# Reordering the start of a selective-scan pass and its handover to an attention pass

## The chip, the cores and the metric

The kernel runs on one core of one Trainium2 chip. A core has five instruction queues: TensorE (PE in the profile), VectorE (DVE), ScalarE (ACT), GpSimd (POOL) and SyncE (SP), which here issues all DMAs. The engines work side by side and wait for each other by semaphores. The metric is the device time of one execution, in microseconds (us).

## The reference

One decoder layer on x of 8 sequences of 512 tokens with 256 features, in float32:

```python
x = x + mamba_block(layernorm(x))                    # L0_attn
x = x + cross_attention(layernorm(x), ctx_1024, ...) # 16 heads of 16
x = x + spiking_ffn(layernorm(x))

def mamba_block(x):
    x_norm = layernorm(x)
    y = (mamba(x_norm, "f") + flip(mamba(flip(x_norm), "b"))) / 2
    x = x + y
    return x + w2 @ gelu(w1 @ layernorm(x) + b1) + b2

def mamba(x):                                        # inner width 512, 16 states
    xi, z = split(x @ in_w.T)
    u = silu(causal_conv4(xi) + conv_b)
    dt, B, C = split(u @ xp_w.T)
    delta = softplus(dt @ dt_w.T + dt_b)
    h[t] = exp(delta[t] * A) * h[t-1] + delta[t] * u[t] * B[t]
    y[t] = sum_n h[t, n] * C[t, n] + u[t] * D
    return (y * silu(z)) @ out_w.T
```

## The kernel before

There are two passes. The first, `mamba_pass`, does the two scans of each sequence. The second, `attention_pass`, does the block's feed-forward part, the cross attention and the spiking part. The first writes its result to DRAM (`mid`), the second loads it.

**Scan pass.** A unit is one sequence in one direction, 16 in all; a loop body holds two units. A unit is 4 blocks (`k`) of 128 channels by 8 pairs of states, 32 steps `p`. A step is:

- `decay` on ScalarE: two exponentials dA of 128x511, from delta.
- `spread_du` on TensorE: the products delta·u·B into a PSUM `pair` bank. 16 small matmuls take `duT` (the transposed product delta·u) and `diagB[:, j]`, diagonals that hold B of the pair j.
- `scan` on VectorE: two scans of 128x512, from dA and the pair bank into h.
- `weigh` on GpSimd: h times the broadcast C (`C_rep`) into hC; `sum_states` on TensorE sums hC into `y_bank`.

The next unit's projections stand between the steps, at places given by small tables (`XI_AT`, `Z_AT` and so on). Three PSUM banks (`general`) are handed out in turn by a `Ring`, along a list of keys (`mamba_keys`, `attention_keys`): a key's first matmul waits until the key before it in that bank has been read.

**Ahead of the loop** stands the first unit's preparation, written out in order on every engine: load x, normalise it twice (VectorE has the statistics, GpSimd the root, ScalarE the scaling), transpose, project xi (keys `xi`, 0 to 3) and gate's z (`z`, 0 to 3), convolve (`start_conv` on ScalarE, three `tap`s on VectorE), silu of all of u and all of z (`silu`), `x_proj`, copy xd (`take_xd`), B (`take_bt`), delta (`soft`, `make_delta`), the product du (`make_du`) and its transposes (`du_rows`, `take_du`). Eight diagonals are made, four on ScalarE (32 small activations) and four on GpSimd. The next unit's first blocks are projected too: z 0 to 2 and xi 0 (keys `("z", 4)` to `("z", 6)` and `("xi", 4)`). At last comes the first spread. Before its loop TensorE waits until the last three keys of the list are read.

**Handover.** At the end of the scan pass TensorE works ahead on the first sequence's feed-forward part (`first_up`, with `first_gelu` on ScalarE), projects the last output (`out_proj`), VectorE adds it to `res` (`add_out`) into `x_out`, and SP stores it as the last slot of `mid`. Each of the five engines then adds one to `handover`, and each waits for all five before it starts on the attention pass. There VectorE first sets constants (`ones_bf`, three rows of `k_st`, `v_sb`), adds the feed-forward result (`add_down`), normalises (`xn_q`), and prepares q, k and v and the masks. SP writes q and k, each cut into three bf16 parts (`cut_lo`, `cut_last`), to DRAM in six DMAs and reads them back in stacked form (`stacks`). After that TensorE starts the loop: `prescore` is a head's four score tiles, of which VectorE takes the maxima with `mask_bias`. `x0` (also `x_mid`) and `xn` belong to the next sequence's feed-forward part, normalised by `first_norm(1)`. `start_x1n` and `take_x1` are sums of 128x1024 on GpSimd.

## Time and profile before

| | |
|---|---|
| median of 3 runs | 2777.25 us (2776.8 to 2777.51) |
| the profiled execution | 2776.59 us, span 2774.8 us |
| TensorE busy | 2633.1 us, 95% |
| VectorE busy | 2203.8 us, 79% |
| ScalarE busy | 1743.1 us, 63% |
| GpSimd busy | 1715.4 us, 62% |
| granted TensorE clock, mean | 0.98 of full |

The span runs from the first instruction to the last. Busy shares are averages over stages with different limits. A line of the timeline is a start, a length, the engine and line of the code, what is written from what, how often, and in brackets the idle time ahead of it with what ended it. A matmul of float32 data shows as two instructions. All instructions made by a helper carry the helper's line: L467 and L471 are the scan pass's matmuls and transposes, L698 its activations, L1325 and L1333 the attention pass's matmuls and transposes, L1236 its DMA issues.

### The profile page before, as it was taken

The numbers are of one execution on the slowest core, as the hardware profiler recorded it, in microseconds if no ns is written. First come the engines' busy times: TensorE is split into PE (matmuls) and PEld (weight loads), VectorE is DVE, ScalarE is ACT, GpSimd is POOL, SyncE is SP. The second block draws the span as 40 slices with busy tenths as digits, with TensorE's granted clock in tenths as the row PEclk, the third lists the DMA queues.
The fourth block names the chain that finished last, engine by engine and source line by source line (L and its number), as shares of the span: only waits on it lengthen the run. The fifth ranks groups of instructions, "written<-read, shape, count | busy, mean of one in ns | idle before, by whom it ended". The sixth has DMA issues, their size and how long they took to land. (4 is left out here: it accounts for less than half of the span.)

```text
span 2774.8 us, 55530 instructions
## 1 busy us (share of the span) xinstructions
PE 2633.1 (95%) x19210; PEld 1798.9 (65%) x19210; DVE 2203.8 (79%) x3271; ACT 1743.1 (63%) x2899; POOL 1715.4 (62%) x962
## 2 busy tenths in 40 slices
PE   5999999999999999999999878999999999999996
PEld 2787787787787778877887744455554545454523
DVE  3999999999999899999999959584848484858573
ACT  4778878877877888788778423535354544444342
POOL 1898989988988998899899812323233232323130
PEclk9999999999999999999999989999999999999978
DMA  3122121302221221222122052304040404040300
GB/s 122 33 80 81 63 65 65 103 28 78 88 67 54 79 81 48 79 66 95 36 77 101 9 158 78 99 25 116 8 121 2 121 2 121 2 121 2 106 2 15
DMA packets 102089, 187.07 MB, mean 67 GB/s; under 512 B 14720, under 2 KB 75264, under 8 KB 100256
## 3 DMA queue, kind: packets, MB, share of 16 engines
q1 hardware_dynamic: 101840, 183.92, 21.3%
q8 instruction: 135, 2.21, 0.3%
q14 instruction: 114, 0.93, 0.1%
HBM read 148.38 MB, written 35.52 MB: 66 GB/s over the span
## 5 line engine op out<-in xcount | busy, mean ns | idle before, releaser
L1087 POOL TENSOR_TENSOR hC<-h,C_rep 128x1024 f32<-128x1024 f32 x512 | 1201.3, 2367 | 100.6 <-DVE h L945 94.1
L945 DVE TENSOR_TENSOR_SCAN h<-dA,pair 128x512 f32<-128x512 f32 x1024 | 1171.3, 1201 | 107.8 <-PE pair L467 96.5
L698 ACT ACTIVATE dA<-delta,cols 128x511 f32<-128x511 f32 x1024 | 664.1, 711 | 41.7 <-DVE h L945 28.3
L467 PE MATMUL pair<-diagB,duT 64*128 64x128 f32 x8192 | 549.0, 281 | 23.4 <-DVE h L945 15.2
L467 PEld LDWEIGHTS pair<-diagB,duT 64*128 64x128 f32 x8192 | 486.2, 188 | 124.5 <-issue 92.7
L558 PE MATMUL y_bank<-ident,hC 128*128 128x128 f32 x4112 | 537.3, 277 | 5.5 <-POOL hC L1087 4.5
L558 PEld LDWEIGHTS y_bank<-ident,hC 128*128 128x128 f32 x4112 | 456.3, 141 | 97.7 <-issue 55.7
L1820 DVE CUSTOM_DVE_ANT_0 masked<-pair,mask_bias 128x512 f32<-128x512 f32 x512 | 322.2, 686 | 19.1 <-PE pair L1325 13.5
L1563 ACT ACTIVATE pr<-pair 128x1024 f32<-128x1024 f32 x256 | 248.3, 1021 | 74.3 <-PE pair L1325 74.3
L1922 POOL CAST m_part<-m_rest 8x512 bf16<-8x512 f32 x16 | 9.6, 602 | 429.1 <-ACT m_rest L1563 429.1
L467 PE MATMUL general<-xnT,w_in 128*128 128x512 f32 x512 | 250.5, 605 | 10.9 <-ACT zs L698 5.1
L1944 POOL TENSOR_TENSOR pr<-pr,keep_word 128x512 int32<-128x512 int32 x112 | 163.9, 1466 | 116.5 <-ACT pr L1563 114.2
L1325 PE MATMUL general<-w_down,g 128*128 128x256 f32 x1024 | 232.5, 380 | 2.8 <-DVEq L1655 2.8
L1325 PEld LDWEIGHTS general<-w_down,g 128*128 128x128 f32 x1024 | 193.7, 190 | 34.8 <-issue 3.8
L1325 PE MATMUL pair<-q_st,k_st 99*128 99x512 bf16 x512 | 196.2, 383 | 3.5 <-ACT pr L1563 3.5
L1325 PE MATMUL general<-xT,w_up 128*128 128x512 f32 x360 | 168.3, 605 | 1.2 <-ACT xT L1563 0.7
L1325 PE MATMUL pair<-k_st,q_st 96*128 96x512 bf16 x512 | 151.5, 404 | 9.1 <-DMA q_st<-qk_parts 6.2
L955 DVE SCALAR_TENSOR_TENSOR u<-general,cols,u 128x511 f32<-128x511 f32 (+2 forms) x192 | 141.9, 739 | 22.8 <-ACT u L698 18.8
L1325 PE MATMUL pair<-mask_biasT,ident_bf 128*128 128x512 bf16 x400 | 152.6, 382 | 0.0
L1893 POOL TENSOR_SCALAR rstd<-mv 128x4 f32<-128x4 f32 x24 | 15.6, 650 | 199.0 <-DVE mv L1670 196.4
L1325 PEld LDWEIGHTS pair<-q_st,k_st 99*128 99x128 bf16 x512 | 50.1, 98 | 135.9 <-ACT pr L1563 91.0
L1078 POOL TENSOR_TENSOR ab<-delta,u 128x512 f32<-128x512 f32 x64 | 82.0, 1281 | 81.6 <-DVE delta L936 81.6
(177 smaller groups left out, 3166.8 us busy)
## 6 DMA issues: line engine op xcount, KB each, us to landing
C_rep<-c_rows SPq DMA_DIRECT2D x128, 512.0 KB, 4.3
qk_parts<-qk_part SPq DMA_DIRECT2D x96, 256.0 KB, 3.9
w_in<-w_in SPq DMA_DIRECT2D x16, 1024.0 KB, 4.9
k_st<-qk_parts SPq DMA_DIRECT2D x8, 1536.0 KB, 9.1
q_st<-qk_parts SPq DMA_DIRECT2D x8, 1536.0 KB, 9.2
x_in<-x SPq DMA_DIRECT2D x18, 512.0 KB, 5.3
w_out<-w_out SPq DMA_DIRECT2D x17, 512.0 KB, 4.2
mid<-x_out SPq DMA_DIRECT2D x9, 512.0 KB, 4.7
```

Of the source, the lines that this page charges most:

```text
L467: return pe.matmul(o, lhsT, rhs, start=start, stop=stop)
L558: last = pe.matmul(y_bank[:, c * P:(c + 1) * P], hC[:, g % RING, i, c * P:(c + 1) * P], ident[:, :], start=j == 0 and i == 0 and c == 0, s ...
L698: return act.activation(o, i, fn, **kw)
L945: last = dve.tensor_tensor_scan(h[:, g % 4, i, :], dA[:, g % 4, i, :], dBu[:, i, :], 0.0, ALU.mult, ALU.add)
L955: dve.scalar_tensor_tensor(u[n][:, k, lag:T], raw[:, 0:T - lag], col("fb"[n] + "conv_w", CW * k + CW - 1 - lag), u[n][:, k, lag:T], ALU.mu ...
L1078: pool.tensor_tensor(ab[:, :], delta[:, k % 2, :], u[par][:, k, :], ALU.mult).then_inc(s_du.sem, 1)
L1087: pool.tensor_tensor(hC[:, g % RING], h[:, g % 4], C_rep[:, 2 * j:2 * j + 2, :], ALU.mult).then_inc(s_hC.sem, 1)
L1325: return pe.matmul(o, lhsT, rhs, start=start, stop=stop)
L1563: return act.activation(o, i, fn, **kw)
L1820: dve.tensor_tensor_reduce(masked[:, j % 2, :], bank[j], mask_bias[:, j, :], 1.0, FLOOR, ALU.add, ALU.max, m_col[:, j, hd:hd + 1]).then_in ...
L1893: pool.tensor_scalar(rstd[:, :], mv[:, :, 1], EPS, None, ALU.add)
L1944: pool.tensor_tensor(words, words, keep_word[:, unit % 2, :].unsqueeze(1).broadcast_to((P, len(heads), T)), ALU.mult).then_inc(s_kept.sem, 1)
```

## The change

No loop body is changed in what it computes or in its order; one wait is added in VectorE's attention code for the first sequence. Parts of the start of the scan pass and of the handover stand in another order or on another engine.

- Start: VectorE negates A_log behind the first statistics. Gate's four blocks of the first unit go to the four `pair` banks, off the ring. ScalarE applies silu to u block by block, and `x_proj` waits for each block (`first_silu`). All eight diagonals are made by GpSimd, two of them ahead of du. The second unit's first blocks `("xi", 4)` and `("z", 4)` are projected ahead of du's transposes, `("z", 5)` and `("z", 6)` behind the first spread, and ScalarE copies those two between its first decays.
- Handover: the last output projection and its two adds move into the attention pass (`last_out` on TensorE, `add_last` on VectorE, keys `lo`), the store behind the stacks of q and k. The ones in `k_st` are written by ScalarE. In `attention_keys` v's projection comes last, behind q's. VectorE's preparation stands in another order. `take_x1(0)` waits until `mask_bias` is set. `yT`, `w_out` and `res` outlive the first pass, so some tiles of the second lie at other addresses; `mask_i` now lies on `x1` and `x_res`.

TensorE from the first projections to the first spread, before and then after. The names: `general` and `pair` are PSUM banks; `xnT` is the normed input, `xd_sb` the result of x_proj, `ab` du, `hC` the states' sums (zero here).

```order
L467 MATMUL general<-xnT,w_in 128x512 x16
L467 MATMUL general<-u_64,w_xp 64x256 x8
L471 MATMUL general<-ident,xd_sb 128x128 x4
L467 MATMUL general<-xd_sb,w_dt 128x512
L467 MATMUL general<-xnT,w_in 128x512 x8
L467 MATMUL y_bank<-hC,ident 128x512
L471 MATMUL general<-ident,ab 128x128 x4
L467 MATMUL pair<-diagB,duT 128x64x2 x8
```

```order
L475 MATMUL general<-xnT,w_in 128x512 x6
L475 MATMUL pair<-xnT,w_in 128x512 x4
L475 MATMUL general<-xnT,w_in 128x512 x2
L475 MATMUL pair<-xnT,w_in 128x512 x4
L475 MATMUL y_bank<-hC,ident 128x512
L475 MATMUL general<-u_64,w_xp 64x256 x8
L479 MATMUL general<-ident,xd_sb 128x128 x4
L475 MATMUL general<-xd_sb,w_dt 128x512
L475 MATMUL general<-xnT,w_in 128x512 x4
L479 MATMUL general<-ident,ab 128x128 x4
L475 MATMUL pair<-diagB,duT 128x64x2 x8
L475 MATMUL general<-xnT,w_in 128x512 x4
```

The z blocks stand in pair banks between the xi blocks, the matmul on `y_bank` has moved ahead of x_proj, and two of the next unit's four blocks (of two matmuls each) have moved behind the spread.

ScalarE in the same stretch, before and then after. `u_64` and `zs_63` are u and z of the forward direction, `zs_65` z of the backward one.

```order
L698 ACTIVATE u_64<-general,cols 128x512 x4
L698 ACTIVATE zs_63<-general 128x512 x4
L698 ACT_TABLE_LOAD
L698 ACTIVATE u_64<-u_64 128x2048
L698 ACTIVATE zs_63<-zs_63 128x2048
L732 ACT_TABLE_LOAD
L698 ACTIVATE xd_sb<-general,cols 64x256 x2
L698 ACTIVATE BT<-general 64x4x16 x2
L698 ACTIVATE ab<-general 128x512
L698 ACTIVATE ab<-ab 128x512 x2
L698 ACTIVATE diagB<-eye,BT 128x64 x32
L698 ACTIVATE zs_65<-general 128x512 x3
```

```order
L718 ACTIVATE u_64<-general,cols 128x512 x3
L718 ACTIVATE zs_63<-pair 128x512 x2
L718 ACT_TABLE_LOAD
L718 ACTIVATE u_64<-u_64 128x512
L718 ACTIVATE u_64<-general,cols 128x512
L718 ACTIVATE zs_63<-pair 128x512
L718 ACTIVATE u_64<-u_64 128x512
L718 ACTIVATE zs_63<-pair 128x512
L718 ACTIVATE u_64<-u_64 128x512 x2
L718 ACTIVATE zs_63<-zs_63 128x2048
L862 ACT_TABLE_LOAD
L718 ACTIVATE xd_sb<-general,cols 64x256 x2
```

The one silu of 128x2048 on u became four of 128x512, which stand between the copies; the 32 activations on `diagB` are gone.

TensorE over the handover, before and then after; the unconditional branches are the boundary of the two passes.

```order
L467 MATMUL pair<-xT_57,w_up_54 128x512 x10
L467 MATMUL general<-w_out,yT 128x256 x16
L330 UNCONDITIONAL_BRANCH
L1320 UNCONDITIONAL_BRANCH
L1325 MATMUL general<-w_down_53,g_58 128x256 x32
L1325 MATMUL general<-ctxT,w_att 128x512 x2
L1325 MATMUL y_bank<-ctxT,w_att 128x512 x2
L1325 MATMUL general<-w_att,ctxT 128x256 x8
L1325 MATMUL pair<-keep_bf,ones_bf 128x512 x4
L1333 MATMUL general<-ident,xn_q 128x128 x4
L1333 MATMUL y_bank<-ident,xn_q 128x128 x4
L1325 MATMUL general<-xT_57,w_att 128x512 x4
```

```order
L1364 UNCONDITIONAL_BRANCH
L1369 MATMUL general<-w_down_53,g_58 128x256 x32
L1369 MATMUL general<-ctxT,w_att 128x512 x2
L1369 MATMUL y_bank<-ctxT,w_att 128x512 x2
L1369 MATMUL general<-w_out,yT 128x256 x8
L1377 MATMUL general<-ident,xn_q 128x128 x8
L1369 MATMUL pair<-keep_bf,ones_bf 128x512 x4
L1369 MATMUL y_bank<-xT_57,w_att 128x512 x2
L1369 MATMUL general<-xT_57,w_att 128x512 x2
L1369 MATMUL general<-w_out,yT 128x256 x8
L1369 MATMUL general<-w_att,ctxT 128x256 x4
L1369 MATMUL y_bank<-w_att,ctxT 128x256 x4
```

The 16 matmuls on `w_out` stood ahead of the boundary and stand in two groups of 8 behind it; those of v (`w_att,ctxT` 128x256) moved to the end.

The diff, cut to its core:

```diff
-    before = many("w2", 2) + many("k", KD) + many("v", 2) + many("qn", KD) + many("q", KD)
+    before = many("w2", 2) + many("k", KD) + [("lo", 0)] + many("qn", KD) + many("q", KD) + [("lo", 1)] + many("v", 2)
...
-    before = [("nf", k) for k in range(KD)] + [("xi", k) for k in range(KI)] + [("z", k) for k in range(KI)]
+    before = [("nf", k) for k in range(KD)] + [("xi", k) for k in range(KI)]
     before += [("xd", 0), ("bt", 0), ("dt", 0)]
-    before += [("z", KI + k) for k in range(KI - 1)] + [("xi", KI), ("tr", 0)]
+    before += [("xi", KI), ("z", KI), ("tr", 0)] + [("z", KI + k) for k in range(1, KI - 1)]
...
+            def first_z(k):
+                for kk in range(KD):
+                    last = mm(bank[k][:, :], w_in[:, kk, DI + k * P:DI + (k + 1) * P], xnT[:, kk, :], kk == 0, kk == KD - 1)
+                last.then_inc(G.full_sem(("z", k)), 1)
...
+                if isinstance(b, str) and b == BEFORE:
+                    pe.wait_ge(first_silu.sem, first_silu.count(kk))
+                elif kk == 0:
                     pe.wait_ge(u_silu.sem, u_silu.count(X))
...
+            du_rows(0, 0, 0, BEFORE)
+            pe.wait_ge(kinds["z"][1].sem, kinds["z"][1].count(KI - 1))
+            spread_du(0, 0)
+            for k in range(1, KI - 1):
                 for kk in range(KD):
                     in_proj(("z", KI + k), 1, 0, k, kk, BEFORE)
...
-            for jj in range(TT // 2):
-                for half in range(2):
-                    out_proj(jj, half, TT + jj, 2 * B - 1, AFTER)
             settle(pe)
             pe.sem_inc(handover.sem, 1)
...
+            for k in range(2):
+                first_z(k)
+            first_u(0)
+            start_conv(KI - 1, 0, 0, KI - 1, BEFORE)
+            first_z(2)
+            first_u(1)
+            first_z(3)
+            for k in range(2, KI):
+                first_u(k)
+            act.wait_ge(kinds["z"][1].sem, kinds["z"][1].count(KI - 1))
+            f(zs[0][:, :, :], zs[0][:, :, :], ACT.Silu).then_inc(z_silu.sem, 1)
+            act.preload_act_table_set("natural_log_exp_and_others")
...
-            for j in DIAG_ACT:
-                diagonals(0, j)
-            for k in range(KI - 1):
-                take_z(KI + k, 1, 1, k, BEFORE)
             start_conv(KI, 1, 1, 0, BEFORE)
+            take_z(KI, 1, 1, 0, BEFORE)
             take_du(0, 0, 0, BEFORE)
+            act.wait_ge(setup.sem, setup.count(0))
+            decay(0, 0, 0)
+            take_z(KI + 1, 1, 1, 1, BEFORE)
+            decay(0, 0, 1)
+            take_z(KI + 2, 1, 1, 2, BEFORE)
+            decay(0, 0, 2)
...
-            for jj in range(TT // 2):
-                dve.wait_ge(s_mid.sem, s_mid.count(B - 1))
-                add_out(jj, TT + jj, x_out, AFTER)
...
+            def first_diagonals(js):
+                for j in js:
+                    made = diag_pool if j in DIAG_POOL else diag_act
+                    pool.wait_ge(kinds["bt"][1].sem, kinds["bt"][1].count(0))
+                    pool.tensor_tensor(diagB[:, j], eye_all(), b_all(j), ALU.mult).then_inc(made.sem, 1)
+            first_diagonals((0, 1))
             make_du(0, 0, 0)
-            for j in DIAG_POOL:
-                diagonals(0, j)
+            first_diagonals(range(2, NP))
...
-            sp.wait_ge(early.mid.sem, early.mid.count(B))
             x_used(0)
             load_x(1)
             dma(s_mask, mask_i[:, :, :], a["mask"].rearrange("(j p) t -> p j t", p=P))
             stacks(0, 0)
             stacks(1, 0)
+            sp.wait_ge(kinds["lo"][1].sem, kinds["lo"][1].count(1))
+            dma(early.mid, mid[B * TT:(B + 1) * TT].rearrange("j p f -> p j f"), early.tiles[0][:, :, :])
...
+            act.wait_ge(s_ones.sem, s_ones.count(0))
+            f(k_st[6 * DH:QR, :, :].rearrange("p h (c e) -> p (h c) e", e=P),
+              ones_bf[6 * DH:QR, :].unsqueeze(1).broadcast_to((3, H * TT, P))).then_inc(k_ones.sem, 1)
...
-            dve.memset(k_st[6 * DH:QR, :, :], 1.0)
...
+            dve.drain()
+            take_q(BEFORE)
+            cut_lo(0, 1)
+            dve.tensor_scalar(keep[:, :, :], maskT_i[:, :, :], 0.0, MASKED, ALU.is_equal, ALU.mult)
+            cut_last(0, 1)
+            add_last(1)
+            first_norm(1)
+            dve.drain()
+            dve.tensor_tensor(mask_biasT[:, :, :], keep[:, :, :],
+                              not_full[:, :].unsqueeze(1).broadcast_to((P, TT, T)), ALU.mult)
             for jj in range(TT // 2):
                 take_v(jj, BEFORE)
...
+            pool.wait_ge(setup_dve.sem, setup_dve.count(1))
             take_x1(0)
```

## Rows read from the trace of the kernel before

**Rows 1.** Scan-loop stretches (width; PE, PEld, DVE, ACT, POOL busy; clock; DMA; GB/s).
```profile
69.30:165.00 95.70, 92.61 (x889) 75.56 (x890) 89.21 (x103) 78.64 (x142) 82.50 (x45) 1.00 0.20 64
...
261.00:357.00 96.00, 93.61 (x895) 75.97 (x894) 89.51 (x102) 78.40 (x142) 86.22 (x48) 1.00 0.23 74
```

**Rows 2.** Issues of the first microsecond (size, us to landing); VectorE's timeline (start, us).
```profile
x_in<-x SPq DMA_DIRECT2D x1, 512.0 KB, 4.0
...
6.45 1.40 DVE L912 BATCH_NORM_STATS2 stats<-x_in 128x6 f32<-128x256 f32 x4
```

**Rows 3.** Timeline of ScalarE and TensorE, gate's projections to xd.
```profile
30.64 0.78 ACT L698 ACTIVATE u<-general,cols 128x512 f32<-128x512 f32 x1 [0.94 <-PE general L467]
...
32.35 0.78 ACT L698 ACTIVATE u<-general,cols 128x512 f32<-128x512 f32 x1 [0.94 <-PE general L467]
...
41.89 1.28 ACT L698 ACT_TABLE_LOAD   x1
43.18 1.91 ACT L698 ACTIVATE u<-u 128x2048 f32<-128x2048 f32 x1
...
45.19 3.62 PE L467 MATMUL general<-u,w_xp 128*64 128x256 f32 x16 [4.07 <-issue]
...
48.91 0.95 ACT L698 ACTIVATE xd_sb<-general,cols 64x256 f32<-64x256 f32 x2 [0.71 <-PE general L467]
```

**Rows 4.** Timeline of the diagonals, and the stretch of the blocks behind them.
```profile
53.50 7.73 ACT L698 ACTIVATE diagB<-eye,BT 128x64 f32<-128x64 f32 x32
...
55.64 4.72 POOL L1093 TENSOR_TENSOR diagB<-eye,BT 128x512 f32<-128x512 f32 x4
...
62.00:66.00 4.00, 4.00 (x6) 1.68 (x7) 0.00 (x0) 0.97 (x3) 0.00 (x0) 0.54 0.55 224
```

**Rows 5.** Timeline of TensorE and VectorE, first pairs of the loop.
```profile
71.75 1.16 PE L467 MATMUL pair<-diagB,duT 64*128 64x128 f32 x16 [0.79 <-DVE h L945]
...
76.45 1.16 PE L467 MATMUL pair<-diagB,duT 64*128 64x128 f32 x16
...
78.45 4.54 DVE L945 TENSOR_TENSOR_SCAN h<-dA,pair 128x512 f32<-128x512 f32 x4
```

**Rows 6.** Timelines at the handover: last gelu on ScalarE, first attention matmul on TensorE.
```profile
1610.15 0.69 ACT L698 ACTIVATE g<-pair,cols 128x512 f32<-128x512 f32 x1 [1.03 <-PE pair L467]
...
1619.81 14.05 PE L1325 MATMUL general<-w_down,g 128*128 128x256 f32 x64 [2.79 <-DVEq L1655]
```

**Rows 7.** Timelines of TensorE and of SP's queue; last row an issue's landing.
```profile
1645.08 5.37 PE L1325 MATMUL general<-xT,w_att 128*128 128x512 f32 x8 [2.59 <-DVE v_sb L1713]
...
1644.36 3.47 SPq L1236 DMA_DIRECT2D qk_parts<-qk_part  x6
1650.75 0.33 SPq L1236 DMA_DIRECT2D k_st<-qk_parts  x1
1655.96 3.46 SPq L1236 DMA_DIRECT2D qk_parts<-qk_part  x6
1663.93 0.33 SPq L1236 DMA_DIRECT2D q_st<-qk_parts  x1
...
q_st<-qk_parts SPq DMA_DIRECT2D x1, 1536.0 KB, 9.3
```

**Rows 8.** Timeline of VectorE, between handover and prescores.
```profile
1638.95 1.38 DVE L1677 TENSOR_SCALAR xn_q<-x1n,mv,rstd 128x256 f32<-128x256 f32 x4 [1.30 <-POOL rstd L1895]
...
1659.52 5.51 DVE L1677 TENSOR_SCALAR xn<-x_mid,mv,rstd 128x256 f32<-128x256 f32 x4 [1.64 <-POOL rstd L1895]
1665.13 3.33 DVE L1801 TENSOR_SCALAR keep<-mask_i 128x2048 f32<-128x2048 int32 x1
```

**Rows 9.** Timelines of TensorE and VectorE, first head of the prescores.
```profile
1673.33 1.89 PE L1325 MATMUL pair<-k_st,q_st 96*128 96x512 bf16 x4 [6.20 <-DMA q_st<-qk_parts]
...
1679.21 1.88 PE L1325 MATMUL y_bank<-xT,w_up 128*128 128x512 f32 x4
...
1676.46 0.63 DVE L1820 CUSTOM_DVE_ANT_0 masked<-pair,mask_bias 128x512 f32<-128x512 f32 x1
```

More of the change, by code:

```diff
@@ L169, in batch @@
         return keys
-    return before, apart(batch(4)), apart(batch(2) + [("yb", 2 * KI)] + [("op", TT + jj) for jj in range(TT // 2)])
+    return before, apart(batch(4)), apart(batch(2) + [("yb", 2 * KI)])
 BEFORE, AFTER = "before", "after"
@@ L988, in add_out @@
                                   ALU.add).then_inc(G.done_sem(("op", i)), 1)
+            first, second = norm_steps(0)
+            for fn in first:
+                fn()
             dve.wait_ge(a_log.sem, a_log.count(0))
@@ L994, in _ @@
             last.then_inc(setup.sem, 1)
-            first, second = norm_steps(0)
-            for fn in first:
-                fn()
             dve.memset(hC[:, :, :, :], 0.0)
@@ L1122, in _, with attention_pass @@
             pool.sem_inc(handover.sem, 1)
-def attention_pass(nc, ctx, a, mid, out, sb, where, stage, psum, consts, handover, early):
+    return Late(yT, w_out, res)
+def attention_pass(nc, ctx, a, mid, out, sb, where, stage, psum, consts, handover, early, late):
     f32, bf16, i32 = mybir.dt.float32, mybir.dt.bfloat16, mybir.dt.int32
@@ L1478, in spike_input, with last_out @@
                 last.then_inc(G.full_sem(key), 1)
+            def last_out(jj):
+                key = ("lo", jj)
+                pe.wait_ge(*G.free(key, BEFORE))
+                bk = G.bank(key, BEFORE)
+                for half_ in range(2):
+                    j = 2 * jj + half_
+                    for k in range(KI):
+                        last = mm(bk[:, half_ * D:(half_ + 1) * D], late.yT[:, k, j * P:(j + 1) * P], late.w_out[:, k, :],
+                                  k == 0, k == KI - 1)
+                last.then_inc(G.full_sem(key), 1)
             pe.wait_ge(early.down.sem, early.down.count(0))
```

99 lines of the change are left out of this document (55 added, 44 removed).

## The prediction

> **What bounds the kernel now.** Read first the page's busy shares: TensorE is busy 95% of the span, the others 62 to 79%. Then stretches of the scan loop: 96 us from the first scan on and 96 us two units later look alike, TensorE busy 92.6 and 93.6 us, at the full granted clock [rows 1]. So the loop runs at its own pace from its first pair on. The change touches no loop body of either pass; what it saves ahead of a loop moves the whole loop, and is kept to the end if the loop starts in the same pattern. Only two serial stretches matter, then: the start (0 to 78 us) and the handover from scan to attention (1610 to 1679 us). There I read the timelines engine by engine, and at each start what released it.
>
> **The start, step by step.**
> - The first statistics. x_in is the first load (issued at 0.8) and lands 4.0 later, at 4.8; VectorE begins at 6.45, behind the negation of A_log [rows 2]. The negation moves behind the statistics: up to 1.6 earlier. The memset of hC then ends about when ScalarE's first normed tile is ready, so I take 1.5, for all as far as the third xi block (its copy moves from 30.64 to 29.1).
> - Projections. Blocks leave TensorE 1.71 apart (30.64 and 32.35) [rows 3]. In the pair banks gate's blocks wait for no general bank: z0 is ready at 30.9, z1 32.6, xi3 34.3, z2 36.0, z3 37.7. ScalarE copies z1 until 33.2, loads its table (1.28) until 34.5, then alternates silu of one block (0.65 each, a third of the 1.91 for four since part of that is fixed) with conv3 (0.78) and two copies (0.6): silu u0 ends 35.1, u1 37.2, u2 38.9, u3 39.6. Gate's silu (1.9) and the second table load end at 42.8. TensorE's x_proj (3.62) runs beside, 38.4 to 42.0. So xd is copied from 42.8 instead of 48.91: 6.1 gained. ScalarE is last here, by 0.8.
> - Diagonals and du. ScalarE worked 7.73 on its four diagonals, three copies of z came after, TensorE stood waiting for these and did the next blocks at a granted clock of 0.54, the 1.2 GHz level [rows 4]. Now ScalarE makes none. GpSimd makes eight at 1.18 (4.72 for four): two from 45.3, du from 48.3 to 49.6 (6.8 behind xd's copy, as before), six until 56.7. Each is ready ahead of its spread; the last one only holds GpSimd's first weighing, at 56.7 instead of 71.7. du's transposes end at 50.3, its copy at 51.0, and the first scan starts at about 52.4 instead of 69.3.
> - What is given back. z5 and z6 are now projected behind the first spread and copied between decays: z5's copy starts at 54.1, decay 1 ends 56.0, z6's copy 56.6. TensorE waits for that copy ahead of its loop, and behind this wait every spread of the loop is queued. With 0.8 for entering the loop (an estimate from the 0.8 of issue that stood ahead of spread 1 before) spread 1 starts at 57.4, spread 2 at 58.5 against 71.75, spread 3 4.70 later, as before: 63.2 against 76.45 [rows 5]. Its scan starts at 64.5 instead of 78.45, 14.0 earlier. TensorE's own chain is 13.3 earlier at spread 3 and 13.6 at spread 4, which no longer waits. I take 13.7. Had all followed the first scan it would be 16.9; were each silu and copy 0.15 dearer and the loop entered 0.5 later, about 12. Bounds 12 to 16.
>
> **The handover.**
> - The last gelu ends at 1610.84, attention's first matmul starts at 1619.81 [rows 6]: out_proj, its two adds and the store of x_out stand between. They go behind the handover, and TensorE's down projection starts 8.4 earlier, at 1611.4. The loads issued at the handover move with it. Setting three rows of k_st to one moves from VectorE to ScalarE: four times the 2048-column pass is 7.6 us, and ScalarE has nothing to do until k is projected, behind the down projection's 14 us: nothing.
> - k. Its parts are cut 8.3 earlier (1636.1), the read of k_st is issued at 1642.4 instead of 1650.75 [rows 7].
> - q. Its projection started at 1645.08 after waiting 2.59 for VectorE's copy of v, and took 5.37 with one more wait. Now it takes banks that are free earlier, and v comes last: it starts when the normed query is copied, 1635.2, and ends 3.4 later, 1638.6. last_out(0), 3.5 us, lies in the time in which TensorE waited for the normed query; last_out(1) behind q. Cutting q followed 5.5 behind the projection's end, so it ends at 1644.2 instead of 1655.96: 11.7.
> - The queue. q's six writes ended at 1663.93, 4 us behind the end of k_st's read (1650.75 plus 9.2, the like read of q_st taking 9.3). Two loads issued right behind q_st's read didn't lengthen it [rows 7]. Both look like one queue served in order. So now k_st lands at 1651.7, q's writes end at 1655.7, q_st lands 9.3 later at 1665.0, against 1673.3: only 8.3; 3.4 of q's gain is lost in the queue.
> - VectorE. Beside GpSimd's sums the four rows of xn took 5.51 and keep 3.33, alone the four of xn_q 1.38, and the other keep of this size takes 1.2 [rows 8]. take_x1 now waits behind mask_bias, so GpSimd is quiet: 6.2 less. From q's cut to the first maximum it was 20.5; less 6.2, and 5.0 more for last_out's add, mask_biasT, v and keep_word, 19.3: ready at 1663.5 instead of 1676.46. The transfer is last now, no longer VectorE.
> - Into the loop. TensorE began the prescores at 1673.33, VectorE joined at 1676.46 [rows 9], and TensorE waited for it in the second head. Now VectorE is there first and TensorE sets the pace (from the lower clock again after some 9 idle us). The second head's prescores are done at 1670.2 instead of 1679.21: **9.0**. Without the last 0.7 it is 8.3; were VectorE last still, 1676.46 to 1663.9 would be 12.6. Bounds 8 to 12.6.
>
> One rule bears on the moved take_x1. The Trainium skill, "SBUF — State Buffer", on who interferes with whom, says that VectorE and GpSimd share a port pair as an exclusive lock, the loser blocked for the whole instruction. The trace agrees (5.51 for four rows beside GpSimd, 1.38 alone). [...]
>
> The sum: 2776.6 (the profiled execution; its span is 2774.8) - 13.7 - 9.0 = 2753.9. The median of the runs is 0.66 above that execution, so the time is 2754.5. At the bounds: 2777.25 - 28.6 = 2748.7 and 2777.25 - 20 = 2757.3.
>
> **Rivals.**
> 1. The queue isn't in order: q's writes share the engines with k_st's read and end 6.4 behind their start, as k's did (1644.36 to 1650.75 [rows 7]). q_st lands at 1660 and VectorE is last: 12.6 instead of 9.0, 2751.0. Against it: the reading of the queue above. Chance 0.15. The Trainium skill, "DMA: Bandwidth & Descriptors", on HWDGE ordering, says that each DMA engine consumes descriptors in ring order but that completion is not first-in first-out; the trace goes with the first half.
> 2. TensorE falls to the lower level in the start. Before, 4.07 idle us ahead of x_proj left it fast [rows 3], some 5 ahead of the later blocks did not (0.54 [rows 4]). The gaps forecast are 2 us or less, but more of them. At the lower level x_proj costs 3.6 more, the two blocks ahead of du hold it up by 2.5, and z5 with z6 cost 2 to 3: the start gives 5 instead of 13.7, time 2763. A part of it gives 2757 to 2760. Chance 0.13 for both.
> 3. Slower. The first pairs enter the loop with another distance (12.1 us from scan 0 to scan 3, where it was 9.15), and the loop keeps a worse pattern, TensorE and VectorE waiting for each other at each pair. It decides from 22.7 us over 512 pairs, 44 ns a pair; at 100 ns it costs 51 and the time is 2806. Against it: the two stretches of [rows 1] are alike although one comes from the start and the other from a loop's end. Chance 0.04.
> 4. The change doesn't do what it says: a load that doesn't move (C_rep, weights) absorbs it, 2772 to 2782. Against it: C_rep is issued 6 us earlier, at 45.8, and first used at 56.7. Chance 0.04.
>
> The forecast has 0.64. Range 2748.5 to 2761: the forecast, rival 1 and the mild half of rival 2. About 0.2% (5.5 us) is what a measurement of this kernel tells from no change: faster 0.93 (forecast, rivals 1 and 2, part of 4), same 0.03, slower 0.04.
>
> **What would show it.** In the profile after: xd copied at 42.8 with two table loads ahead of it, not more; scan 0 near 52.4 and spread 3 near 63; 53.6 us (before 53.5) between attention's first matmul and its first prescore, which q_st's read releases; q's writes 11.4 us long, not 8; xn at 0.35 a row. I am wrong in the start if scan 0 comes early and spread 3 doesn't, in the handover if VectorE or k_st's constants are last, and altogether if a unit of the loop isn't 95.8 us.

## The result and the profile after

The kernel after takes 2754.98 us (median of 6 runs, 2752.52 to 2756.8), the kernel before beside it 2777.2: a ratio of 0.992, 95% interval 0.9908 to 0.9932. In a later set of runs (run 12 below) it was 2754.68 (5 runs) against 2777.3, ratio 0.9918 (0.9904 to 0.9931). 2754.5 was forecast.

| profiled execution | before | after |
|---|---|---|
| time, span | 2776.59, 2774.8 | 2753.38, 2751.6 |
| xd copied from | 48.91 | 41.28 |
| scan 0, scan 3 | 69.30, 78.45 | 52.98, 64.83 |
| spread 3 | 76.45 | 63.55 |
| last gelu's start | 1610.15 | 1597.75 |
| attention's first matmul | 1619.81 | 1599.01 |
| first prescore | 1673.33 | 1651.71 |
| second head's up projection | 1679.21 | 1657.31 |

**The start.** ScalarE's timeline (start, length) beside [rows 3]: the first table load, silu of the first block of u, the second table load, the copy of xd.

```profile
32.01 1.28 ACT L718 ACT_TABLE_LOAD   x1
...
33.30 0.63 ACT L718 ACTIVATE u<-u 128x512 f32<-128x512 f32 x1
...
39.99 1.28 ACT L862 ACT_TABLE_LOAD   x1
41.28 0.95 ACT L718 ACTIVATE xd_sb<-general,cols 64x256 f32<-64x256 f32 x2
```

Two table loads as before, but the first comes 9.9 earlier and silu starts on one block. Then TensorE, from x_proj to spread 3, in the places of [rows 3, 4, 5] (after x_proj: xd's transposes, dt, the two blocks, the first spread, spreads 1 and 2, spread 3):

```profile
37.29 1.95 PE L475 MATMUL general<-u,w_xp 128*64 128x256 f32 x16
...
42.38 1.10 PE L479 MATMUL general<-ident,xd_sb 128*128 128x128 f32 x4 [3.14 <-ACT xd_sb L718]
43.27 1.92 PE L475 MATMUL general<-xd_sb,w_dt 81*128 81x512 f32 x2
44.98 5.30 PE L475 MATMUL general<-xnT,w_in 128*128 128x512 f32 x8
...
51.71 1.16 PE L475 MATMUL pair<-diagB,duT 64*128 64x128 f32 x16 [0.96 <-ACT duT L718]
...
57.95 2.06 PE L475 MATMUL pair<-diagB,duT 64*128 64x128 f32 x32 [1.45 <-ACT zs L718]
...
63.55 2.06 PE L475 MATMUL pair<-diagB,duT 64*128 64x128 f32 x32
```

and the granted clock of that stretch (the number behind the busy times of PE, PEld, DVE, ACT and POOL):

```profile
41.00:46.00 5.00, 3.62 (x8) 2.10 (x9) 0.00 (x0) 2.45 (x7) 1.84 (x2) 0.56 0.57 170
46.00:51.00 5.00, 4.75 (x12) 2.06 (x10) 1.71 (x3) 2.57 (x5) 3.54 (x4) 0.76 1.01 329
```

TensorE stood idle for 3.14 us ahead of the transposes and came back at the 1.2 GHz level: dt took 1.92, the two blocks 5.30. x_proj took 1.95, where it took 3.62 before [rows 3]. Both are 16 instructions of one form, and in the loop it takes 1.95 as well. The granted clock under the 3.62 of before:

```profile
45.20:48.80 3.60, 3.60 (x16) 1.87 (x16) 0.00 (x0) 2.97 (x2) 0.00 (x0) 0.53 0.49 175
```

So before the change x_proj ran at the lower level, behind 4.07 idle us. VectorE's scans:

```profile
52.98 2.33 DVE L981 TENSOR_TENSOR_SCAN h<-dA,pair 128x512 f32<-128x512 f32 x2 [0.65 <-PE pair L475]
...
64.83 4.55 DVE L981 TENSOR_TENSOR_SCAN h<-dA,pair 128x512 f32<-128x512 f32 x4 [0.39 <-PE pair L475]
```

Scan 0 is 16.3 earlier, scan 3 13.6, spread 3 12.9.

**The loop.** In the stretches of [rows 1] TensorE is now busy 94.3 and 94.6 us (92.6 and 93.6), the clock at 1.00. The higher number comes from where the window falls: in the 95.7 us from the first scan on, as in the first of [rows 1], it is 92.8. Its pace is best read from the loads of w_in, one for each unit; the first and last start of these on SyncE, before and then after:

```profile
L337 SPq DMA_DIRECT2D w_in<-w_in x16: 373/383/434, 2.8 to 1365.1; - x16
```

```profile
L346 SPq DMA_DIRECT2D w_in<-w_in x16: 373/384/434, 2.8 to 1352.6; - x16
```

Of the sixteen, fourteen are issued in the loop, from 119.64 before and from 106.03 after. That is 95.81 us a unit before and 95.89 after. So the 13.6 us by which the first of these loads is earlier are 12.46 at the last, and the last gelu is 12.4 earlier. The missing 1.2 is taken up again below.

**The handover.** Last gelu, then TensorE at the down projection, the q projection (its first row), the first prescore and the second head's up projection, beside [rows 6, 7, 9]:

```profile
1597.75 0.69 ACT L718 ACTIVATE g<-pair,cols 128x512 f32<-128x512 f32 x1 [1.03 <-PE pair L475]
```

```profile
1599.01 14.05 PE L1369 MATMUL general<-w_down,g 128*128 128x256 f32 x64 [1.29 <-DVEq L1717]
...
1622.77 1.98 PE L1369 MATMUL y_bank<-xT,w_att 128*128 128x512 f32 x4 [1.09 <-ACT xT L1622]
...
1651.71 1.88 PE L1369 MATMUL pair<-k_st,q_st 96*128 96x512 bf16 x4 [7.95 <-DMA q_st<-qk_parts]
...
1657.31 1.88 PE L1369 MATMUL y_bank<-xT,w_up 128*128 128x512 f32 x4
```

SyncE's issues, beside those of [rows 7], and VectorE's xn, keep and first maximum, beside [rows 8, 9]:

```profile
1623.57 3.48 SPq L1279 DMA_DIRECT2D qk_parts<-qk_part  x6
1629.55 0.33 SPq L1279 DMA_DIRECT2D k_st<-qk_parts  x1
1631.99 3.19 SPq L1279 DMA_DIRECT2D qk_parts<-qk_part  x6
1642.63 0.33 SPq L1279 DMA_DIRECT2D q_st<-qk_parts  x1
```

```profile
1636.16 1.38 DVE L1739 TENSOR_SCALAR xn<-x_mid,mv,rstd 128x256 f32<-128x256 f32 x4 [1.64 <-POOL rstd L1967]
...
1642.00 1.23 DVE L1871 TENSOR_SCALAR keep<-mask_i 128x2048 f32<-128x2048 int32 x1
...
1652.50 0.69 DVE L1890 CUSTOM_DVE_ANT_0 masked<-pair,mask_bias 128x512 f32<-128x512 f32 x1 [1.53 <-issue]
```

The down projection starts 20.8 earlier, which is the 12.4 of the last gelu and 8.4. q is projected 22.3 earlier (1622.77 against 1645.08), but q's writes need 10.6 from issue to end, and q_st's read, the last thing that TensorE waits for (7.95 idle), lets it go only 21.6 earlier. VectorE's four rows of xn took 1.38 (before 5.51), keep 1.23 (3.33).

**The end.** The store of the last but one sequence's output is issued at 2683.43 (before 2705.07), 21.6 earlier; from there to the end it is 68.2, before 69.7.

### The profile page after: what moved, and what is told of

The parts are those of the page before. It is cut to its first block and busy times, and to the rows that moved or that the text cites. A ratio compares the mean times of both kernels' runs of the same rounds, so it can differ in the third digit from the quotient of the medians.

```text
span 2751.6 us, 55456 instructions
## 1 busy us (share of the span) xinstructions
PE 2626.7 (95%) x19177; PEld 1797.4 (65%) x19210; DVE 2191.5 (80%) x3270; ACT 1743.0 (63%) x2871; POOL 1720.0 (63%) x966
## 5 line engine op out<-in xcount | busy, mean ns | idle before, releaser
L475 PE MATMUL pair<-diagB,duT 64*128 64x128 f32 x8192 | 549.7, 281 | 23.3 <-DVE h L981 13.7
L475 PE MATMUL general<-xnT,w_in 128*128 128x512 f32 x496 | 242.0, 603 | 4.5 <-ACT xnT L718 3.6
L1369 PE MATMUL pair<-mask_biasT,ident_bf 128*128 128x512 bf16 x368 | 140.6, 382 | 0.0
L1369 PEld LDWEIGHTS pair<-k_st,q_st 96*128 96x128 bf16 x512 | 50.2, 98 | 116.4 <-DVE m_col L1890 82.1
```

The costliest lines, as they stand in the source:

```text
L475: return pe.matmul(o, lhsT, rhs, start=start, stop=stop)
L1369: return pe.matmul(o, lhsT, rhs, start=start, stop=stop)
```

## The experiments

Runs of one chip are compared with each other: before took 2778.0 beside the first four kernels, 2776.63 beside the next four, 2777.3 beside the last. The kernel after alone spread over 4.3 us in its six runs, so where a kernel has a single run (3, 4, 6, 7, 8) its time says little, and the argument rests on its profile. A profile is one execution: kernels with the same code up to there copied xd at 40.81 (run 4) to 42.38 (run 8).

**1. The start alone.** The handover stands as before.

```
- attention_keys, last_out, add_last, take_x1's wait   (as in the kernel before)
+ first_silu, first_z, first_diagonals, z5/z6 behind the first spread   (as in the kernel after)
```

> The start's changes alone; the handover as before. If the gain is the sum of two independent stretches, spread 3 stands at 63.5 as in the changed kernel (76.45 before), the time is 2777.2 less 12.4 to 13.6: 2763.6 to 2764.8, and the stretch from last gelu to the second head's products is as before (68.4 us from 1610.84 to 1679.21). Rival, one part needs the other: then it is more than 1.5 us outside this. A second question: w_in's issues in the scan loop were 13.6 earlier in unit 0 and 12.5 earlier in the last one. If the start's pattern costs this, it is here too; if it belongs to single executions, it may be absent.

Measured: 2766.79 (5 runs, 2766.15 to 2767.28), ratio 0.996 (0.9946 to 0.9974): 11.2 less than before, where 12.4 to 13.6 were expected. Spread 3 stands at 63.50, as in the kernel after, and from the last gelu's end to the second head's up projection it is 68.5 us (before 68.4). The difference went later: the last w_in is issued at 1353.47, only 11.6 earlier than before (95.96 us a unit), and the down projection follows it by 255.9, before by 254.7.

**2. The handover alone.** The start stands as before.

```
+ attention_keys, last_out, add_last, take_x1's wait   (as in the kernel after)
- first_silu, first_z, first_diagonals, z5/z6 behind the first spread   (as in the kernel before)
```

> The handover's changes alone; the start as before. Sum of two stretches: down projection 8.4 behind the last gelu less than before, prescores 9.2 earlier, second head's products 9.5 earlier, time 2767.7 (2767 to 2768.7). Rival, one part needs the other: over 1.5 us outside. The scan loop's w_in issues then stand where they stood before (119.6 and 1365.1); if they drift here by 1 us as well, the drift is not the start's.

Measured: 2768.4 (6 runs, 2767.63 to 2769.4), ratio 0.9965 (0.9953 to 0.9978): 9.6 less. The down projection follows the last w_in by 246.4 (before 254.7): the 8.3 to 8.4 again. Counted from there, the first prescore is 9.1 earlier, as expected, and the second head's up projection 8.4, not 9.5: its first up projection ran at the lower clock (3.62). The loop stands at 95.81 us a unit, so the 0.09 belongs to the start. The two parts give 20.8 when added, both together 22.2, a difference that the intervals don't resolve.

**3. Silu of u in one piece again.**

```
-            first_u(0)
             start_conv(KI - 1, 0, 0, KI - 1, BEFORE)
             first_z(2)
-            first_u(1)
             first_z(3)
-            for k in range(2, KI): first_u(k)
+            act.wait_ge(s_tap.sem, ...)
+            f(u[0][:, :, :], u[0][:, :, :], ACT.Silu).then_inc(first_silu.sem, KI)
```

> Silu on all of u in one activation again, and x_proj behind it, gate's blocks still in the pair banks. Theory (ScalarE is last here): the table load comes after z3's copy (37.1) unless the taps are later, u's silu 1.9 from 38.4 to 40.3, gate's 42.2, table 43.5; x_proj 40.3 to 42.3; so xd is copied at 43.5 instead of 41.28, 2.2 later, and the time is 2757. Rival, TensorE is last: x_proj ends before that and nothing beyond the two table loads matters, xd within 1 us of 41.28.

Measured: 2753.61 (one run), within the spread of the kernel after. ScalarE's copy of xd and TensorE's spread 3:

```profile
43.64 0.95 ACT L718 ACTIVATE xd_sb<-general,cols 64x256 f32<-64x256 f32 x2
```

```profile
64.93 2.06 PE L475 MATMUL pair<-diagB,duT 64*128 64x128 f32 x32
```

The step is right (xd 2.36 later, spread 3 1.38 later) and the time didn't follow. The last w_in comes at 1352.73, level with the kernel after's 1352.65: its loop took 95.79 us a unit, the other's 95.89, and 13 such units are the 1.3. So silu in blocks won nothing in the end.

**4. Four diagonals on ScalarE again.**

```
             soft(0, 0, 0, BEFORE)
+            for j in DIAG_ACT:
+                diagonals(0, j)
...
-            first_diagonals((0, 1))
             make_du(0, 0, 0)
-            first_diagonals(range(2, NP))
+            first_diagonals(DIAG_POOL)
```

> Four diagonals on ScalarE again (32 activations, 7.7 us), between delta's logarithm and the copy of xi 4; GpSimd makes four, behind du. Theory: copies of xi 4, z 4 and of du all wait for them: ScalarE is free at 47.2 + 7.7 = 54.9, du's copy ends about 57, scan 0 starts at 58 instead of 53.0, spread 3 about 5 later, time 2759.5 to 2760.5. Rival, the diagonals were hidden anyway behind du on GpSimd (done at 49.3): less than 2 us.

Measured: 2758.97 (one run), 4.0 more than the kernel after. TensorE ahead of its first spread:

```profile
55.05 2.08 PE L475 MATMUL pair<-diagB,duT 64*128 64x128 f32 x16 [6.67 <-ACT duT L718]
```

It waits 6.67 for ScalarE's copy of duT, which stands behind 7.76 us of diagonals. Scan 0 comes at 57.24 (4.3 later) and spread 3 at 69.48 (5.9 later). Of these 5.9 the faster loop returns 1.5 again (last w_in 4.4 later).

**5. The second table load behind the copies of xd.**

```
-            act.preload_act_table_set("natural_log_exp_and_others")
             act.wait_ge(s_zero.sem, s_zero.count(0))
             take_xd(0, BEFORE)
+            act.preload_act_table_set("natural_log_exp_and_others")
```

> The kernel after with one edit: ScalarE's second table load stands behind its copies of xd instead of ahead of them. Theory (after's trace: silu of z ends 39.97, the table load takes 1.28, xd is copied at 41.28, while x_proj ended at 39.2; TensorE then stood idle for 3.14 and did the next matmuls at the lower clock, dt's two in 1.92): the load is all that ScalarE holds up. xd is copied at 40.0, and TensorE idles 1.8 instead of 3.1. If the clock stays high with that, dt takes 1.0 and the two blocks 3.6, and scan 0 starts at about 50.8, time 2752.3. Rival: the clock falls as before; everything moves by 1.3 alone, scan 0 at 51.7, spread 3 at 62.3, time 2753.7. Second rival: GpSimd's diagonals hold spread 3 at 63 in any case, time as after (2755).

Measured: 2752.72 (4 runs, 2751.67 to 2755.05), ratio 0.9914 (0.9896 to 0.9932). The copy of xd, then TensorE's transposes and dt:

```profile
40.07 0.94 ACT L718 ACTIVATE xd_sb<-general,cols 64x256 f32<-64x256 f32 x2
```

```profile
41.15 0.72 PE L479 MATMUL general<-ident,xd_sb 128*128 128x128 f32 x4 [1.71 <-ACT xd_sb L718]
41.71 1.02 PE L475 MATMUL general<-xd_sb,w_dt 81*128 81x512 f32 x2
...
48.66 1.99 PE L475 MATMUL pair<-diagB,duT 64*128 64x128 f32 x16 [0.94 <-ACT duT L718]
50.58 4.49 PE L475 MATMUL general<-xnT,w_in 128*128 128x512 f32 x8
...
62.11 2.06 PE L475 MATMUL pair<-diagB,duT 64*128 64x128 f32 x32
```

The clock stays high after 1.71 idle us, dt takes 1.02 and scan 0 comes at 50.76, as expected for that case. But spread 3 gains 1.44 only. The lower level came later instead: the first spread took 1.99 (1.16 in the kernel after), and z5 with z6 4.49 (3.70), together 1.6 more. In run 11, with the same edit, these took 1.16 and 3.70, and spread 3 came at 59.74. Between the two runs the distance from xd's copy to spread 3 differs by the same 1.6. The time is 2.3 below the kernel after's 2754.98 of another set of runs, and the ranges of both overlap.

**6. Without z5 and z6.**

```
-            take_z(KI + 1, 1, 1, 1, BEFORE)
+            act.wait_ge(...); act.sem_inc(...)      # and on TensorE in_proj left out, the same for z6
             decay(0, 0, 1)
```

> Leaves out part of the computation: the second unit's gate blocks z5 and z6 are neither projected nor copied; their semaphores are stepped. It asks what gave back the difference between scan 0 (16.3 earlier than before) and spread 3 (12.9 earlier). Theory of the prediction: z5's and z6's projections (3.70) and copies do; without them spread 1 follows scan 0 at 53.7 instead of 57.95, and spread 3 would come up to 4.2 earlier, at 59.3. Rival, which I now hold likelier: behind spread 1 stand the sums of the first step, and GpSimd weighs that step only when its six diagonals are made (56.28, weighed at 58.64); so the sums start at 58.9 instead of 60.0, and spread 3 moves by 1.0 only, to 62.5, scan 3 to 63.8. Time 2754, or 2751 by the first theory.

Measured: 2748.78 (one run). TensorE's transposes, dt and spread 3:

```profile
41.91 0.72 PE L479 MATMUL general<-ident,xd_sb 128*128 128x128 f32 x4 [3.14 <-ACT xd_sb L718]
42.47 1.02 PE L475 MATMUL general<-xd_sb,w_dt 81*128 81x512 f32 x2
...
57.77 1.16 PE L475 MATMUL pair<-diagB,duT 64*128 64x128 f32 x16
```

Spread 3 is 5.8 earlier. 2.4 of that were there at scan 0 already (50.60): 0.5 at xd's copy (40.82), and 1.9 because dt and the blocks ran at the full clock although TensorE had been idle for the same 3.14. The other 3.4 are z5 and z6. The forecast's reason for what is given back between scan 0 and spread 3 stands, and the rival that I held likelier falls: the first sums came at 54.16, before GpSimd had weighed anything, so they don't wait for its diagonals. I had read the order of two rows as a dependence.

**7. q's writes ahead of both reads.**

```
+            for n in range(2): (three writes of part n)
+            sp.wait_ge(s_qkw.sem, s_qkw.count(1))
+            (read k_st; read q_st)
-            stacks(0, 0); stacks(1, 0)
```

> The kernel after with SyncE's order changed at the handover: k's three writes, q's three writes, then the two reads k_st and q_st behind each other (after: k writes, k_st read, q writes, q_st read; there q's writes took 10.6 from issue to end, the read before them 9, and q_st's read released TensorE at 1651.7). Theory, the queue is served in order: q's writes end about 6.3 behind their issue at 1632 (as k's do), so 1638.3 instead of 1642.6; both reads are then issued, k_st lands 9.0 later at 1647.3 and q_st 7.4 to 9.3 behind it, 1655 to 1656.6: TensorE's first prescore 3.3 to 5 later than 1651.7. Rival, reads share the sixteen engines: both land together at the end of the same time, which looks alike for the last one, but k_st lands late too, near 1655. A third, reads overlap: q_st lands 9.3 behind its issue, at 1647.6, 4.1 earlier than in after, and then VectorE (ready 1651.0) is last.

Measured: 2757.32 (one run), 2.3 more than after. SyncE's two reads, and TensorE's first prescore:

```profile
1638.26 0.33 SPq L1279 DMA_DIRECT2D k_st<-qk_parts  x1
1638.62 0.43 SPq L1279 DMA_DIRECT2D q_st<-qk_parts  x1
```

```profile
1654.98 1.88 PE L1374 MATMUL pair<-k_st,q_st 96*128 96x512 bf16 x4 [11.38 <-DMA q_st<-qk_parts]
```

q's writes, issued at 1631.9, have ended 6.4 later, not 10.6, when no read is ahead of them. By their landings k_st's read took 9.9 from its issue and q_st's 16.2, 6.7 behind it. That is one queue served in order: reads that share the engines would have landed together, overlapping reads at 1647.6.

**8. GpSimd's sums beside VectorE's preparation.**

```
-            pool.wait_ge(setup_dve.sem, setup_dve.count(1))
             take_x1(0)
+    ScalarE waits for mask_bias in their place; mask_i lies elsewhere, loaded behind w2
```

> The kernel after with GpSimd's sums of the next sequence (take_x1) not waiting for mask_bias: they stand beside VectorE's preparation again, as before the change (the int mask lies elsewhere and is loaded behind w2, and ScalarE's part of the loop waits for mask_bias in their place). Theory (before's trace: xn's four rows took 5.51 and keep 3.33 beside GpSimd; after's 1.38 and 1.23 without): VectorE is 6.2 later, ready at about 1657 instead of 1651.0, behind q_st's landing at 1651.7; the first maxima come at 1657.5 instead of 1652.5, and the second head about 5 later less what GpSimd's earlier end saves; time +3 to +5, 2758 to 2760. Rival: VectorE's slowness in before came from something else (its place in the order, the DMAs into the tiles); then xn takes 1.4 and the time stays at 2755.

Measured: 2758.67 (one run), 3.7 more. VectorE's rows of xn and the second keep:

```profile
1637.06 3.41 DVE L1741 TENSOR_SCALAR xn<-x_mid,mv,rstd 128x256 f32<-128x256 f32 x4 [1.64 <-POOL rstd L1969]
...
1648.60 3.33 DVE L1877 TENSOR_SCALAR keep<-mask_i 128x2048 f32<-128x2048 int32 x1
```

3.41 for 1.38 and 3.33 for 1.23, beside GpSimd's sums at 1637.3 and from 1645.2 to 1650.9. GpSimd, beside the first keep:

```profile
1645.18 3.19 POOL L1979 TENSOR_TENSOR x1n<-x_in,x_mid 128x1024 f32<-128x1024 f32 x1 [5.51 <-DVE keep_word L1869]
```

The first keep had started at 1644.93, ahead of this sum: it took its 1.23, and the sum 3.19 instead of 2.35. The second keep started behind a sum (1648.60 against 1648.51), and here VectorE paid. Whoever started second waited. VectorE's first maximum is 3.4 later (1655.92), 0.9 of it from ahead of the handover. The wait for mask_bias is worth this much, though in the kernel after VectorE isn't what TensorE waits for: without the wait it would be.

**9, 10. Reads cut by heads; then VectorE's closing memsets on GpSimd.**

```
-  read k_st; q's writes; read q_st
+  read k_st[heads 0:8]; q's writes; read q_st[heads 0:8]; read k_st[8:16]; read q_st[8:16]
+  TensorE: if hd == H // 2: pe.wait_ge(s_qkr2.sem, ...)
10: also
-            dve.memset(y_sb[A3], 0.0); dve.memset(x_res[A3], 0.0)
+            pool.memset(y_sb...); pool.memset(x_res...).then_inc(s_clear.sem, 1)
```

> The kernel after with the two reads of the handover cut by heads: heads 0 to 7 of k_st, q's writes, heads 0 to 7 of q_st, and only then heads 8 to 15 of both, for which TensorE waits ahead of head 8 (in every sequence, where it hides behind other work). It asks what it is worth that q_st's read is no longer last. Theory, a queue served in order: half of k_st's read (4.6) is out of q's way, q's writes end near 1638.3 instead of 1642.6, half of q_st lands 4.6 to 6 behind, at 1643 to 1644.5; TensorE is free at 1643.8, VectorE at 1651.0 as in after. VectorE is last then: first maximum 1651.0 instead of 1652.5, the second head's up projection 2.75 behind it as before the change, 1653.8 instead of 1657.3: 3.5 less, time 2751.5. Rival: the halves cost as much as the wholes (the read is bound by its descriptors, or the second halves' reads hold the first up), q_st lands near 1648 or later, gain 1.5 or less. Second rival: what stood last was TensorE itself after its idle 8 us at the lower clock; the gain is then whatever its idle time shrinks by, and it may be the full 5 to 6.

> The kernel of the run before this one (reads cut by heads), with VectorE's two closing memsets of y_sb and x_res (0.91 each, with their waits 2.3 in all) on GpSimd, which is idle there. Theory: VectorE is last there, so its end moves from 1651.0 to 1648.7 and everything with it: 2.3 less than the run before, 2749.3. Rival: with the transfer early, TensorE (free at 1643.8, then prescores and up projection, 5.1 at the full clock, more at the lower) sets the pace, and the memsets are worth less than 1. Second rival, by what early sums on GpSimd did to VectorE (3.33 for a pass of 1.23): the memsets on GpSimd hold VectorE's passes up by as much as they spare it.

Measured: 2752.48 (4 runs, 2751.5 to 2753.29; ratio 0.9912, 0.9897 to 0.9927) and 2751.53 (4 runs, 2748.93 to 2753.83; 0.9907, 0.9892 to 0.9922), beside 2754.68 for the kernel after on the same chip. The first of them, on TensorE:

```profile
1644.49 1.88 PE L1375 MATMUL pair<-k_st,q_st 96*128 96x512 bf16 x4 [1.08 <-DMA q_st<-qk_parts]
...
1653.46 3.62 PE L1375 MATMUL y_bank<-xT,w_up 128*128 128x512 f32 x4
```

The transfer is no longer last: half of q_st has landed at 1644.5, and VectorE finds its first tiles ready when its memsets are done (1650.53). The second head's up projection follows the down projection by 54.8 instead of 58.3: the 3.5 expected, but it takes 3.62 instead of 1.88, at the lower clock, and the next 1000 us are 2 us longer (from there to the last but one sequence's store 1028.2, against 1026.1 in the kernel after); why they are is open. 2.2 is left, with ranges that overlap. In the second kernel VectorE's xn took longer beside the memset on GpSimd:

```profile
1636.34 2.16 DVE L1748 TENSOR_SCALAR xn<-x_mid,mv,rstd 128x256 f32<-128x256 f32 x4 [1.64 <-POOL rstd L1975]
```

2.16 for 1.38: 0.8 of the 2.3 was paid back there. Behind the down projection VectorE is 1.2 earlier, the time 0.95, which the runs don't tell from nothing.

**11, 12. Late table load, cut reads and memsets together (the edits of 5, 9 and 10); and the kernel after again, with no edit.**

> Reads cut by heads, closing memsets on GpSimd, and ScalarE's second table load behind its copies of xd. Theory: the parts lie in different stretches and add up: 3.5 and 2.3 in the handover, 1.4 in the start (spread 3 came at 62.11 with the late table load instead of 63.55): 7.2 less than after, 2747.8. If the handover's parts bring half, 2751.

> The kernel after again, unchanged, on the chip of the three runs beside it, for comparison. Theory: 2755 as before, with a spread of some 4 us that goes with when TensorE's clock comes back at the last sequence's end (in its first profile 1.3 us of its gain stood there). Its scan pass should again take 95.9 a unit from the load of w_in at 106.0 to that at 1352.6; the kernel with the start alone took 95.96, the kernel before 95.8. If it is 95.8 this time, that difference was chance; if again 95.9, the loop has kept a slightly worse pattern, which costs about 1.2 over the pass.

Measured: 2749.06 (4 runs, 2747.29 to 2750.47), ratio 0.9899 (0.9884 to 0.9914), against 2754.68 (5 runs, 2752.15 to 2756.59). 5.6 less than the kernel after (7.2 expected), 28.2 less than before. TensorE at the first prescore and the second head's up projection:

```profile
1642.50 1.88 PE L1376 MATMUL pair<-k_st,q_st 96*128 96x512 bf16 x4 [0.32 <-DMA q_st<-qk_parts]
...
1650.19 1.88 PE L1376 MATMUL y_bank<-xT,w_up 128*128 128x512 f32 x4
```

Here the up projection ran at the full clock (1.88), 53.5 behind the down projection instead of 58.3. In this profile spread 3 is 3.8 earlier than in the kernel after and not 1.4 (see run 5), but the pass's end took 2 us more (below). This is the fastest version of the study. The kernel after took 95.93 us a unit again, so its 95.9 wasn't chance.

## Why the prediction was right

The time was, the steps in part. Their sum; the first rows are those of the two profiled executions, the last two are averages over the profiles named below (in the first pair alone they are 0.8 and 1.6):

| | forecast | measured |
|---|---|---|
| start, at scan 3 | 14.0 | 13.6 |
| start, at spread 3 | 13.3 | 12.9 |
| start, taken | 13.7 | 13.6 (first load of w_in in the loop) |
| loop | 0 | -1.2 |
| handover, to the down projection | 8.4 | 8.4 |
| handover, behind it | 0.6 | 0 on average |
| last sequence's end | 0 | 1.3 |

13.6 - 1.2 + 8.4 + 1.3 = 22.1, and the medians differ by 22.2, where 22.7 were forecast. That the total came so close is in part luck: loop and handover fell 1.8 short, and 1.3 at the end, which the forecast didn't have, made up for most of it.

- **xd.** Forecast 42.8, measured 41.28. u's third block was copied at 28.02, not 29.1, and silu of one block took 0.57 to 0.63. ScalarE was last, as forecast, but by 2.0 instead of 0.8: x_proj ended at 39.24, not 42.0.
- **x_proj was read wrongly.** The forecast took its 3.62 for the full speed, and rival 2 held that the 4.07 idle us of before left TensorE fast. They did not: the granted clock was 0.53 there, and the full-speed length is 1.95. So the lower level would cost it 1.7, not 3.6. The error moved the sum little, because ScalarE was last; but it hid the longer idle time: x_proj ended earlier, and TensorE waited the longer for xd.
- **The clock in the start** was the second rival, in a mild form. Its condition came true: TensorE idled 3.14 (forecast: 2 or less), and dt and the two blocks together took 2.6 longer than at the full clock (1.92 against 1.02, 5.30 against 3.60). At scan 0 it cost 1.9: 11.70 us from xd's copy, against 9.78 in run 6, where the clock stayed high. The 1.5 won at xd paid for most of it, and scan 0 came at 52.98 against 52.4.
- **What is given back** between scan 0 and spread 3: 3.4 of 16.3, for z5 and z6 as forecast (run 6).
- **Rival 3 came true in small**, with the sign and place but not the cause that I gave. The price per unit is 0.09 us (95.89 against 95.80), 1.2 in all; the break-even was 44 ns for a pair, this is 3. Between 158 and 172 us, TensorE's rows of the kernel after and of run 3 are the same to 0.01 us, shifted by 1.45. What differs is one wait of ScalarE in each body, for delta's product. In the kernel after (TensorE's product, ScalarE's copy, then TensorE's spread eight us on with the load that waits for duT):

```profile
162.97 1.02 PE L475 MATMUL general<-xd_sb,w_dt 81*128 81x512 f32 x2
...
171.74 2.37 PE L475 MATMUL pair<-diagB,duT 64*128 64x128 f32 x32
```

```profile
164.36 0.60 ACT L718 ACTIVATE ab<-general 128x512 f32<-128x512 f32 x1 [2.36 <-PE general L475]
```

```profile
172.94 0.97 PEld L475 LDWEIGHTS pair<-diagB,duT 64*128 64x128 f32 x16 [0.23 <-ACT duT L718]
```

and with silu in one piece (run 3), at the same place:

```profile
164.41 1.02 PE L475 MATMUL general<-xd_sb,w_dt 81*128 81x512 f32 x2
...
173.19 2.11 PE L475 MATMUL pair<-diagB,duT 64*128 64x128 f32 x32
```

```profile
165.54 0.60 ACT L718 ACTIVATE ab<-general 128x512 f32<-128x512 f32 x1 [2.08 <-PE general L475]
```

In the first ScalarE starts 1.39 behind the product's start, in the second 1.13, and at the end of the unit the spread takes 2.37 instead of 2.11. All fourteen profiles fall into two groups: nine with 2.35 or 2.36 idle ahead of that copy and 95.88 to 95.96 a unit (after twice, runs 1, 5, 7 to 11), and five with 2.08 and 95.78 to 95.81 (before, runs 2, 3, 4, 6). In the nine ScalarE's program has 70 instructions between its start and the loop, in the five it has others (109 in before and run 2, 106 in run 4, 68 in runs 3 and 6). That points to where the instructions lie, but nothing here tests it; the cause stays open.
- **The handover.** last_out's move is worth the 8.4 of the forecast: from the last w_in to the down projection twelve profiles of kernels with it took 246.4 on average (245.3 to 247.5), before 254.7 and run 1 255.9. q's writes took 10.6 (forecast 11.4), the prescore came 52.7 behind the down projection (53.6; before 53.5), released by q_st's read: the queue in order was right, and rival 1 fell with run 7. What failed is the 0.6 behind it. I compared with a TensorE that waited for VectorE in the second head; what TensorE gained there it lost at the lower clock (3.21 for the first up projection, before 2.76). From the prescore to the second head's up projection it needed 5.60 in the first profile, but 6.34 in the second and 5.8 to 6.6 in runs 2 to 6, where before took 5.88. From the down projection to the store of the last but one sequence's output before took 1085.26 and run 1 1085.25, and seven profiles with the new handover (after twice, runs 2 to 6) took 1084.4 to 1085.9, 1085.35 on average.
- **take_x1's wait.** Right: xn at 0.35 a row, and run 8 shows what it costs without. The Trainium skill, "SBUF — State Buffer", on who interferes with whom, has the engine that comes second blocked for the whole of the other's instruction where VectorE's instruction uses both port pairs, and no contention for one with at most one input in SBUF outside the two-port modes. The traces agree: in run 8 the second keep ended 1.1 behind the sum's end, which is nearly its whole length, and in the kernel after VectorE's closing memsets took their 0.91 beside a sum of 2.34.
- **The end.** Not foreseen: from that store to the end of the span before and run 1 took 69.7 and 69.6, eleven of the twelve profiles with the new handover 68.1 to 68.5 (run 11 70.4). In six stretches of 6 us from that store the granted clock read 1.00, 1.00, 0.85, 0.50, 0.80, 1.00 before and 1.00, 1.00, 0.93, 0.50, 1.00, 1.00 after: by these the lower level lasts some 7 us instead of 10, around the same work. Why it does is open.

## What to carry to other kernels

A sum of two stretches ahead of long loops is a sound way to forecast, because a loop without waits on the changed part keeps its distance; but compare the loop's time per unit too, since a quarter of a microsecond of wake-up in each body took back a twentieth of the gain. Where work before a transfer is sped up, look at what stands ahead of the transfer in its queue: cutting the reads in two and letting only the needed half go first brought the second head 3.5 us forward (2.2 in the time). Look up the granted clock under a row before taking its length for the full speed: x_proj's 3.62 was 1.95. And the clock that TensorE comes back with after idle time is worth 1.6 to 1.9 us in a start like this one, and differed between kernels with the same idle time, so a difference of 2 us between two single profiles there can be the clock alone.

## What the runs showed of the hardware

- The same 3.14 us of idle time ahead of xd's transposes left TensorE at the lower level in most profiles (dt 1.91 or 1.92: the kernel after twice, runs 1, 7, 8, 9, 10) and at the upper in two (1.02: runs 4 and 6). After 1.71 it was at the upper in both kernels that had it (runs 5 and 11), after 1.60 in run 3 at the lower. After 0.94 the first spread of run 5 was at the lower (1.99), that of run 11 at the upper (1.16). So the last idle time alone doesn't decide it.
- Of two reads of 1.5 MB issued 0.36 us apart on one queue the first landed after 9.9 and the second after 16.2, where one with none right ahead of it took 8.9 and 9.1 (both in the kernel after). A read of half the size, with two more behind it, landed 5.7 behind its issue (run 9).
- ScalarE's table load took 1.28 us, and the next activation started 0.01 later.
- GpSimd beside VectorE, both on SBUF: of a keep and a sum that overlap, the later starter took longer (keep 3.33 for 1.23, or the sum 3.19 for 2.35; both in run 8). A tensor_scalar of 128x256 took 0.35 alone, 0.85 (run 8) to 1.38 (before) beside GpSimd's sums and 0.54 beside its memset, on the mean of four. VectorE's memset of 128x1024 took 0.91 alone (v_sb's, 1599.96) and beside a sum (y_sb's and x_res's, 1648.98 and 1650.06, beside GpSimd's from 1648.85 to 1651.2 in the kernel after).
